# A causal mask added by 32-row products in place of full-array products

## The reference

```python
q = (x @ Wq + bq).reshape(B, T, 32, 8).transpose(0, 2, 1, 3)
k = (x @ Wk + bk).reshape(B, T, 8, 8).transpose(0, 2, 1, 3)
v = (x @ Wv + bv).reshape(B, T, 8, 8).transpose(0, 2, 1, 3)
q = q * cos + rotate_half(q) * sin
k = k * cos + rotate_half(k) * sin
scores = jnp.einsum('bhqd,bhkd->bhqk', q, k_rep) / scale
scores = jnp.where((kpos > qpos)[None, None], -jnp.inf, scores)
attn = jax.nn.softmax(scores, axis=-1)
out = jnp.einsum('bhqk,bhkd->bhqd', attn, v_rep)
return out.transpose(0, 2, 1, 3).reshape(B, T, C) @ Wo + bo
```

## Time and profile before

| | |
|---|---|
| Median of 3 runs | 680.17 us (678.83 to 680.18) |
| The profiled execution | 681.94 us |
| Its span, first to last instruction | 680.0 us |
| Mean granted clock of TensorE | 0.915 of full speed |
| First expert layer | about 0 to 204 us |
| Second layer norm and first projections | about 217 to 236 us |
| Attention | about 236 to 503 us |
| Second expert layer | about 503 to 680 us |

### The profile page before, as it was taken

How to read it: one execution, slowest core, us unless ns; L and a number is a source line. 1 busy time by engine, 2 the same in 40 slices (tenths; PEclk the granted TensorE clock), 3 DMA queues, 4 the chain that set the end, 5 groups by cost and what they waited for, 6 DMA issues and landing times.

```text
span 680.0 us, 14568 instructions
## 1 busy us (share of the span) xinstructions
PE 574.7 (85%) x4310; PEld 306.2 (45%) x4310; DVE 512.2 (75%) x1521; ACT 405.3 (60%) x830; POOL 244.9 (36%) x201
## 2 busy tenths in 40 slices
PE   3897488999931898999999999999979998999960
PEld 2353355776620343333322323334334655777750
DVE  6689867885749558888898889887747574888864
ACT  5467657765622457775746777677775334666640
POOL 3388416888862000000000000000012773888880
PEclk9899879999875569999999999999988997999995
DMA  5299897876773067462202220222200334999969
GB/s 179 78 302 351 292 291 135 138 143 119 97 124 124 0 209 219 142 190 79 79 1 80 79 78 1 80 80 79 79 1 19 114 128 113 162 148 150 145 70 263
DMA packets 78299, 87.71 MB, mean 129 GB/s; under 512 B 5905, under 2 KB 72337, under 8 KB 78226
## 3 DMA queue, kind: packets, MB, share of 16 engines
q1 hardware_dynamic: 55104, 54.93, 26.5%
q0 software_dynamic: 16608, 21.77, 19.6%
q10 hardware_dynamic: 6514, 10.10, 4.9%
HBM read 33.15 MB, written 53.62 MB: 128 GB/s over the span
## 4 chain that ended last, share of the span: by engine, by line
PE 60%; DVE 13%; issue 7%; ACT 7%; POOL 6%; DMA 5%; SPq 1%; ACTq 0%; DVEq 0%; POOLq 0%
PE psum L1319 16%; PE psum L1564 10%; PE psum L1534 9%; PE psum L1547 5%; POOL xg_dram L697 5%; PE psum L1530 3%; DVE W_ex L1067 3%; PE psum L1551 3%; PE psum L1367 2%; DVE m_part L1270 2%; DMA acc_dram<-R,add_to 2%; DMA R<-acc_dram 2%; ACT W_ex L738 2%; PE psum L1409 1%; PE psum L1410 1%
## 5 line engine op out<-in xcount | busy, mean ns | idle before, releaser
L1270 DVE TENSOR_REDUCE m_part<-psum 128x1 f32<-128x512 f32 (+3 forms) x304 | 182.3, 655 | 33.0 <-PE psum L1534 31.6
L708 POOL DMA_INDIRECT acc_dram<-R,add_to x94 | 148.9, 1584 | 64.7 <-DVE R L1128 43.8
L883 ACT ACTIVATE R<-psum 128x1024 f32<-128x1024 f32 x144 | 141.1, 1022 | 44.0 <-PE psum L1547 33.3
L1319 PE MATMUL psum<-W_ex,R 128*128 x564 | 105.1, 325 | 4.9 <-ACT R L797 4.7
L724 POOL TENSOR_TENSOR R<-R 128x256 f16<-128x256 f32 x6 | 3.9, 667 | 286.7 <-ACT R L865 286.7
L1534 PE MATMUL psum<-kT,qTs 128*128 128x512 f16 (+3 forms) x384 | 99.1, 332 | 1.9 <-DVE m_part L1270 1.2
L697 POOL DMA_INDIRECT xg_dram<-R,o_tok x64 | 73.0, 1141 | 49.0 <-DVE o_tok L1022 30.1
L1564 PE MATMUL psum<-R,vals 128*32 128x512 f32 x576 | 76.7, 604 | 0.4 <-ACT oT L891 0.2
L1319 PE MATMUL psum<-xT,W_sh 128*128 128x512 f16 x264 | 67.3, 409 | 6.0 <-DVE R L1078 3.1
L1319 PEld LDWEIGHTS psum<-W_ex,R 128*128 128x128 f16 x564 | 52.6, 101 | 28.5 <-issue 6.6
L811 ACT ACTIVATE R<-R 128x176 f16<-128x176 f32 x94 | 32.9, 350 | 47.1 <-DVE R L1098 45.9
(11 more groups left out here) (196 smaller groups left out, 1002.4 us busy)
## 6 DMA issues: line engine op xcount, KB each, us to landing
xg_dram<-pad_sb SPq DMA_DIRECT2D x16, 1296.0 KB, 6.6
R<-xg_dram SPq DMA_DIRECT2D x88, 144.0 KB, 3.1
kT<-w_dram ACTq DMA_DIRECT2D x15, 512.0 KB, 5.1
R<-acc_dram SPq DMA_DIRECT2D x24, 256.0 KB, 5.3
acc_dram<-rot_b SPq DMA_DIRECT2D x3, 1152.0 KB, 9.1
acc_dram<-ex SPq DMA_DIRECT2D x6, 576.0 KB, 3.5
xg_dram<-pad_sb SPq DMA_DIRECT2D x17, 144.0 KB
kT<-w_dram SPq DMA_DIRECT2D x4, 384.0 KB, 5.9
```

The costliest lines, as they stand in the source:

```text
L708: nc.gpsimd.indirect_dma_start(acc_dram[f][n % NA], bass.IndirectOffsetOnAxis(ap=add_to[:, n % 8:n % 8 + 1], axis=0), y_sb[:, n % 4, :], N ...
L883: nc.scalar.activation(prob[:, n % 2, 2 * pair:2 * pair + 2, :].rearrange("p g n -> p (g n)"), psum[:, 1024 * pair:1024 * (pair + 1)], ACT ...
L1270: nc.vector.tensor_reduce(m_part[:, h:h + heads, kt // 4], ps, axis=AX.X, op=ALU.max).then_inc(free_of(e), 1)
L1319: ins = nc.tensor.matmul(o, stat(a, k), mov(b, k), start=first and n == 0, stop=last and n == 3 * k_parts - 1, **kw)
```

## The change

The mask of the transposed scores is built from four pieces of 32 queries. For each of the four blocks `b` of 32 query columns, and for each row group of the step, a product of 32 rows adds the mask: its weights are 32 rows of the mask (`mask_rows[rows, b, :]`, 128 keys wide), its moving operand is a 32 by 32 identity repeated for the four query heads (128 columns), and it writes those 128 of the bank's 512 columns. Two products of 512 moving columns become eight of 128.

`mask_rows` holds the mask's four blocks side by side in each of the four row groups. Four more transfers on SP's queue fill its fp32 source, and one more DVE conversion, in the `pj` event of tile 2, writes it to a free place in `R1`. The other mask, `maskb`, keeps only the half that line 1530 uses.

The planner's costs change too: `st` on the diagonal 0.65 to 0.48, `pv` 1.0 to 0.87, and 0.1 for each step of PE from one of three kinds (`st`, `pv`, all else) to another. So the orders in which all engines run the attention's events change with it. `LEAN` stays.

```diff
+SWITCH = 0.1
...
-            return [(PE, 0.65 if diag else 0.22, [("q2", e[3]), ("st", e[1] - 1, e[2])]),
+            return [(PE, 0.48 if diag else 0.22, [("q2", e[3]), ("st", e[1] - 1, e[2])]),
...
-            return [(PE, 1.0, [("st", t, 1), ("o", e[2] - 1), ("pj", e[4])])]
+            return [(PE, 0.87, [("st", t, 1), ("o", e[2] - 1), ("pj", e[4])])]
...
+    mode = {"st": 1, "pv": 2}
...
+        if engine == PE and order[PE] and mode.get(e[0], 0) != mode.get(order[PE][-1][0], 0):
+            begin += SWITCH
...
+        mask_rows = R1[:, 4096:4096 + GLO * P // 2].bitcast(BF16).rearrange("p (b n) -> p b n", b=GLO)
...
-        N_CONST, N_LATE = 2 * 16, 2 * 16
+        N_CONST, N_LATE = 2 * 16, (2 + GLO) * 16
...
-            sp.dma_start(maskf, mask_in).then_inc(s_late, 16)
+            sp.dma_start(maskf, mask_in[:, 0, :]).then_inc(s_late, 16)
+            for gl in range(GLO):
+                sp.dma_start(mask_rows_f[ROW * gl:ROW * (gl + 1)],
+                             mask_in[:, 0, :].rearrange("(b q) n -> q b n", q=ROW)).then_inc(s_late, 16)
...
+                    if t == 2:
+                        link(nc.vector.tensor_copy(mask_rows, mask_rows_f))
...
-                    for gl in (2 * pair, 2 * pair + 1):
-                        if kt == t:
-                            ins = nc.tensor.matmul(bank[gl].rearrange("p (j n) -> p j n", j=GQ), identb[:],
-                                                   maskb[:, 1, :].unsqueeze(1).to_broadcast([P, GQ, P]),
-                                                   start=False, stop=True)
+                    for b in range(GLO if kt == t else 0):
+                        for gl in (2 * pair, 2 * pair + 1):
+                            rows, cols = slice(ROW * gl, ROW * (gl + 1)), slice(ROW * b, ROW * (b + 1))
+                            ins = nc.tensor.matmul(
+                                bank[gl].rearrange("p (j n) -> p j n", j=GQ)[:, :, cols], mask_rows[rows, b, :],
+                                identb[rows, ROW * gl:ROW * (gl + 1)].unsqueeze(1).to_broadcast([ROW, GQ, ROW]),
+                                start=False, stop=b == GLO - 1)
```

More of the change, by code:

```diff
@@ L264, in build @@
         identb = sb("identb", [P, P], BF16)
-        maskb = sb("maskb", [P, 2, P], BF16)
+        maskb = sb("maskb", [P, P], BF16)
         R1 = sb("R1", [P, 2048 + TT * XR], F32)
@@ L314, in build @@
         rot_a = sb("rot_a", [P, NROT, QW + KW], F32)
-        maskf = rot_a[:, 0, 0:2 * P].rearrange("p (a n) -> p a n", a=2)
+        maskf = rot_a[:, 0, 0:P]
+        mask_rows_f = rot_a[:, 2:4, :].rearrange("p a n -> p (a n)")[:, 0:GLO * P].rearrange("p (b n) -> p b n", b=GLO)
         rot_b = sb("rot_b", [P, QW + KW], F32)
@@ L1529, in _ @@
                         ends_at = out_bank[:, 0:heads * n].rearrange("p (h n) -> p h n", h=heads)[:, :, n - P:n]
-                        nc.tensor.matmul(ends_at, identb[:], maskb[:, 0, :].unsqueeze(1).to_broadcast([P, heads, P]),
+                        nc.tensor.matmul(ends_at, identb[:], maskb[:].unsqueeze(1).to_broadcast([P, heads, P]),
                                          start=True, stop=False, skip_group_check=True)
```

## The result

The changed kernel is slower. Its median is 687.18 us (683.13 to 688.68, 6 runs) against 679.17 for the kernel before (678.11 to 680.18, 6 runs): ratio 1.0106, 95% interval 1.0074 to 1.0138. The forecast was 671 us, with 664 to 679 as the range.

What follows compares the result with a forecast made beforehand. TensorE was taken to bound the attention, with DVE next. Of 8.3 us saved on masks 6.9 arrive, plus 2.5 from the new order: 9.4 us off the median 680.17, so 671 us, range 664 to 679.

Steps and rivals of the forecast that it cites:

- What bounds the kernel: Attention: TensorE's time is the attention's, 90% of the chain from 302 to 502 us, 68% before; DVE is next.
- The price of the new products: Diagonal steps on TensorE: eight mask products take 0.22 us, a step before full-array work 0.54 instead of 0.76.
- take turns: Rival, diagonal masks: the two row groups do not overlap, masks take 0.45 us, kernel 679 us; chance 0.08.
- bare loads: Rival, diagonal masks: each round waits out a weight load, masks take 0.58 us, kernel 683 us; chance 0.03.
- What arrives of it: Attention: of 8.3 us saved on TensorE, 6.9 us reach the kernel's time, by the chain's shares.
- DVE takes over: Rival, attention: reductions bound more often, only half of 8.3 us arrives, order gives nothing, 676 us; chance 0.18.
- What else is added: Before tile 2's rotation and on SP's queue: conversion at most 0.57 us, four transfers at most 3.7, both priced 0.
- The new order: Planner's order of the attention: 25 fewer changes of shape on TensorE at 0.10 us each, a gain of 2.5 us.
- The rival on the other side: Attention: the new order starves DVE, full-array maximum products wait behind scores and values, 681 to about 690 us; chance 0.09.
- The sign I named myself: Changed kernel's trace: TensorE's idle time before DVE's releases growing by more than 5 us would show the prediction wrong.
- Another sign: Changed kernel's trace: DVE's idle time before line 1270 should shrink by about as much as the attention.

Runs made afterwards that it cites:

- a_old_order: The changed kernel with the three planner costs of before put back, so the new mask products in the old order: 671.47 us against 676.84, ratio 0.9913.
- g_values_first: The changed kernel with a planner bonus of 0.1 for the value event on TensorE: 699.94 us against 676.84, ratio 1.0336.
- f_pv_cost_only: The kernel before with only the planner's cost of the value event lowered from 1.0 to 0.87, no product changed: 704.89 us against 676.84, ratio 1.0408.

## Why the prediction was wrong

- **What bounds the kernel**: right for the old order. TensorE holds 90% of the chain in the later part, and with the order kept most of its saving arrived.
- **The price of the new products**: right. Forecast 0.54 us before full-array work and 0.54 before values; measured 0.54 and 0.55. The two row groups run side by side, and no load lies bare. The rivals "take turns" and "bare loads" fall. The rule of the Trainium skill, page "TensorE: Matmul & The Clock Gate", section "What overlaps and what doesn't", that a weight load overlaps matmuls in flight only when its row group differs, does not hold for these products: the four loads in each row group are hidden in the 0.17 us. Where the two steps of a visit run into each other, the visit is cheaper than forecast, 0.78 us in place of 0.98.
- **What arrives of it**: too large. Forecast were 8.3 us saved on TensorE and 6.9 arriving. With the old order 5.4 us arrived in one comparison (676.84 - 671.47) and 5.8 in the other (677.32 - 671.57), although a little more was saved: without the first visit, the steps of a_old_order take 8.5 us less than those of the kernel before, where 7.7 were forecast. So at most two thirds arrived and not five sixths, which lies between the forecast and the rival "DVE takes over".
- **What else is added**: right. The conversion took 0.426 us (upper end 0.57), and DVE still idled 0.43 us before the next rotation. SP issued the four transfers in 2.13 us (upper end 3.7), under cover. The tile view and SP's timeline of the changed kernel:

```profile
L1244 DVE CAST R<-rot_a x1: 426/426/426, 229.2 to 229.2; 128x512 bf16<-128x512 f32 x1
```

```profile
7.89 2.13 SPq L618 DMA_DIRECT2D rot_a<-mask_dram  x4
```

- **The new order**: this is the step that failed. I gave it a gain of 2.5 us, "25 fewer" changes of shape at 0.10 each. The changes in the written order fell even further, from 312 to 267, 4.5 us at that price. (The 325 that I counted in the trace included changes at the full-array masks; they go with the products and not with the order, since the same count gives some 310 for a_old_order.) But the order as a whole costs 13 us with the new products (1.9% of 677) and 16 us with the old ones. I priced the one thing that the planner's edit names and took everything else about the order as kept. What the runs showed in its place is the path above: long rows of maximum products that go out at the pace of DVE's reductions, 33.0% of the chain in place of 3.9%, with ACT idle meanwhile and its exponentials late.
- **The rival on the other side**, with a chance of 0.09, had the right place and about the right size (10 us or more), and the wrong mechanism for the changed kernel. DVE was not starved there: its idle time before reductions fell from 33.0 to 23.6 us. TensorE stood before maximum products that came too early, ACT ran dry, and at the end ACT's exponentials came late: from 470 to 507 us they hold 23.3% of the chain, in place of 1.0% over the earlier trace rows. DVE was starved in g_values_first.
- **The sign I named myself** came true: TensorE's wait for DVE's releases grew by far more than 5 us (its loads' from 39 to 70). Another sign misled: DVE's idle time was to shrink by about as much as the attention, and it shrank by 9.4 us while the attention grew by 7. So the trace could settle it, but only afterwards. The new order itself could have been written out beforehand, since the planner needs no chip: it has 17 value events behind the last maximum product in place of 6. That count alone does not give the time (g_values_first has 4 and loses too), but it shows that the order had moved. What I also had beforehand was that `LEAN` had been set to quarters of a unit under the old costs, and that 0.1 and 0.13 are of the size of what decides between two ready events. That was ground for a much wider range on the slow side.

The second expert layer took 1.6 us longer in the profile of the changed kernel, though nothing in it changed. That is scatter: from the end of the last logits to the end of the program it is 168.2 us there and 166.6 in the kernel before, and 165.1 to 168.1 in the other profiles beside which the kernel before took its usual time. Left open is why a given order loses as much as it does: the chain shows where the time goes, but nothing here computes the 28 us of f_pv_cost_only or the 13 of the changed kernel.

## What to carry to other kernels

When a change edits the costs or rules of a greedy planner that writes fixed orders, price the order apart from the instructions, and take its effect as unknown in sign: here 0.13 on one cost was worth 28 us, five times the saving on the instructions. Keep the old order (freeze it, or keep the old costs, wrong as they are) to see what the instructions are worth, then look for an order by replaying candidates with the durations of the trace and to the end of the stage that follows (here that gave 668.18 us, the best time, though not clearly ahead of the old order). Two views show a bad order quickest. In the windows view in a few equal stretches no engine is short of work in total, but in each stretch another one is idle. In the chain of what ended last, an engine that was not the limit holds long unbroken pieces.

## What the runs showed of the hardware

Products of 32 rows in different row groups overlap across the steps, not only within one: the second pair's scores started 0.01 us after the first pair's first masks (496.66 and 496.67), and a whole diagonal visit took 0.78 us, where its two steps one behind the other would be 0.44 + 0.54 = 0.98. Four products with their own weights in the same row group went out within 0.17 us (eight pass in 0.38, one alone in 0.21). That is 0.056 from one to the next, what 128 columns take anyway (0.22 / 4), so the loads added nothing.
